# Differences for an adjacency's one-hots: formed on GpSimd for two chunks at once, squared on ScalarE in one instruction

## What is computed

```python
def sage_conv(x, edge_index, W_l, b_l, W_r):
    src, dst = edge_index
    agg = segment_sum(x[src], dst, num_segments=x.shape[0])
    cnt = segment_sum(ones, dst, num_segments=x.shape[0])
    return (agg / max(cnt, 1)[:, None]) @ W_l.T + b_l + x @ W_r.T

x = x + sage_conv(relu(sage_conv(layernorm(x), ...)), ...)     # two graph layers
x = x + ffn(layernorm(x))      # router, spatial and temporal attention, cross attention, MLP
```

## Time and profile before

| | |
|---|---|
| time, median of 3 runs | 1835.78 us (1834.69 to 1836.27) |
| the profiled execution | 1835.89 us |
| its span, first to last instruction | 1833.8 us |
| mean granted TensorE clock | 0.961 |
| busy share: TensorE / weight load / VectorE / ScalarE / GpSimd | 91% / 75% / 61% / 48% / 40% |
| chain that ended last, by engine | PE 73%, DVE 11%, ACT 5%, POOL 4%, issue 3%, DMA 3% |
| the stage of the 83 groups | about 51.5 to 157.6 us |

### The profile page before, as it was taken

The page is one execution under the profiler, slowest core; times in us unless marked ns, Lnnn a source line. Parts: engine busy times, 40 slices in busy tenths (PEclk is TensorE's granted clock), DMA queues, the critical chain, the costliest instruction groups (busy, mean ns, idle before and its releaser), DMA issues.

```text
span 1833.8 us, 27123 instructions
## 1 busy us (share of the span) xinstructions
PE 1659.9 (91%) x9904; PEld 1376.7 (75%) x9904; DVE 1126.7 (61%) x1802; ACT 882.2 (48%) x1728; POOL 725.0 (40%) x593
## 2 busy tenths in 40 slices
PE   2898999849999999988999997999999997699997
PEld 1566776438788888866878996778888885488876
DVE  7995124630588889851048887228888886843332
ACT  3894322312388788722127775108888774311100
POOL 3122020033634455032367873354535556433431
PEclk9998999969999999988999998999999998899999
DMA  3000000131212112033123321321112120011111
GB/s 105 7 24 24 0 29 18 61 131 39 47 29 57 29 29 52 1 97 136 34 60 65 62 53 64 107 62 29 29 34 52 35 80 18 18 35 40 40 40 56
DMA packets 33000, 88.40 MB, mean 48 GB/s; under 512 B 5190, under 2 KB 5660, under 8 KB 32369
## 3 DMA queue, kind: packets, MB, share of 16 engines
q1 hardware_dynamic: 32881, 86.83, 17.3%
HBM read 43.29 MB, written 12.80 MB: 31 GB/s over the span
## 4 chain that ended last, share of the span: by engine, by line
PE 73%; DVE 11%; ACT 5%; POOL 4%; issue 3%; DMA 3%; DVEq 1%; SPq 0%; POOLq 0%; ACTq 0%
PE ps L902 11%; PE ps L687 11%; PE ps L688 11%; PE ps L689 11%; PE ps L883 10%; PE ps L868 7%; PE ps L869 6%; PE ps L808 2%; DMA w_raw<-in_weights 1%; PE ps L809 1%; DVE R L1341 1%; DVE stats L1298 1%; POOL F L604 1%; PE ps L918 1%; ACT F L1077 1%
## 5 line engine op out<-in xcount | busy, mean ns | idle before, releaser
L549 POOL TENSOR_TENSOR w_hi<-w_raw,zero 128x512 fp32r<-128x512 f32 x96 | 109.7, 1142 | 723.8 <-PE ps L689 456.0
L1090 ACT ACTIVATE R<-ps 125x500 fp32r<-125x500 f32 (+3 forms) x632 | 291.1, 508 | 148.1 <-PE ps L883 146.7
L1542 DVE TENSOR_REDUCE TB<-ps 125x1 f32<-125x1250 f32 (+4 forms) x240 | 299.4, 1262 | 83.0 <-PE ps L869 57.4
L1551 DVE TENSOR_TENSOR R<-ps,R 125x500 fp32r<-125x500 f32 (+3 forms) x632 | 324.0, 568 | 11.0 <-ACT R L1090 10.9
L1077 ACT ACTIVATE F<-ps,TB 125x1250 f32<-125x1250 f32 (+4 forms) x240 | 275.9, 1157 | 88.6 <-DVE TB L1542 88.6
L902 PE MATMUL ps<-R 125*128 125x252 f32 (+1 forms) x2080 | 288.7, 286 | 2.3 <-DVE F L1594 2.3
L883 PE MATMUL ps<-ident,F 125*125 125x125 f32 x2040 | 259.9, 275 | 8.4 <-ACT F L1077 7.3
L902 PEld LDWEIGHTS ps<-R 125*128 125x128 f32 x2080 | 255.8, 189 | 2.6 <-DVE R L1551 1.6
L687 PE MATMUL ps<-R,w_hi 128*128 128x512 f32 (+1 forms) x576 | 213.5, 371 | 42.6 <-POOL w_lo L564 14.0
L883 PEld LDWEIGHTS ps<-ident,F 125*125 125x125 f32 x2040 | 239.9, 190 | 11.8 <-ACT F L1077 11.5
L868 PE MATMUL ps<-R 128*125 128x512 f32 (+5 forms) x624 | 240.6, 386 | 4.2 <-DVE R L1551 2.9
(11 more groups left out here) (175 smaller groups left out, 2457.5 us busy)
## 6 DMA issues: line engine op xcount, KB each, us to landing
R<-F SPq DMA_DIRECT2D x96, 312.5 KB, 5.2
w_raw<-in_weights SPq DMA_DIRECT2D x96, 256.0 KB, 2.6
TB<-in_x SPq DMA_DIRECT2D x10, 250.0 KB
x_d<-F SPq DMA_DIRECT2D x10, 250.0 KB
zt_d<-F SPq DMA_DIRECT2D x1, 2500.0 KB, 8.6
F<-zt_d SPq DMA_DIRECT2D x1, 2500.0 KB, 13.1
qc_d<-F SPq DMA_DIRECT2D x4, 625.0 KB, 3.9
xt_d<-F SPq DMA_DIRECT2D x4, 625.0 KB, 3.5
```

Of the source, the lines that this page charges most:

```text
L549: return eng.tensor_tensor(to, a, zero[0:to.shape[0], :].to_broadcast(list(to.shape)), ALU.add)
L1090: eng.activation(probs_run(K, n, 0, part, lo, hi), ps[0:P, 3 * (n % 2) + bank, P * (lo - j0):P * (hi - j0)] .rearrange("p (c t) -> p c t", ...
L1542: ins = eng.tensor_reduce(out=ngm[0:P, 2 * (n % 2) + part:2 * (n % 2) + part + 1], in_=flat(n % 2)[0:P, at:at + P * blocks], op=ALU.max, a ...
L1551: eng.tensor_tensor(probs_run(K, n, 1, part, lo, hi), ps[0:P, 3 * (n % 2) + bank, P * (lo - j0):P * (hi - j0)] .rearrange("p (c t) -> p c ...
```

## The change

GpSimd forms the difference (position + loT) for both chunks of a group in one instruction of 125x2x128, from two broadcast inputs, and writes it as bf16 to `sq_lo`. ScalarE squares it in place, both chunks in one instruction of 256 columns, and goes on as before. GpSimd's addition for group g waits until ScalarE's one-hots of group g-2 have freed the buffer (`lo_ready`); ScalarE's square waits for the addition (`lo_away`, new). The cuts of units 4 to 9 are now placed between the additions: units 4 to 7 behind those for groups 38 to 41, units 8 and 9 behind those for groups 78 and 79; the cuts from unit 10 on come after the last addition.

```diff
+        unit_ok, lo_away = sem("unit_ok"), sem("lo_away")
 @ gpsimd
             eng.memset(F[0:P, 0:5120], 0.0).then_inc(at_zero, 1)
-            cut_units(4, UNIT["us"])
+            def distances(g):
+                if g >= 2:
+                    eng.wait_ge(lo_ready, g - 1)
+                    eng.sem_inc(held, 1)
+                eng.tensor_tensor(sq_lo[:, g % 2, :, :], iota_b[:, 0:128].unsqueeze(1).to_broadcast([P, EA, 128]),
+                                  loT[:, EG * g:EG * g + EA].unsqueeze(2).to_broadcast([P, EA, 128]), ALU.add
+                                  ).then_inc(lo_away, 1)
+            eng.wait_ge(e.ev, 2)
+            eng.sem_inc(held, 1)
+            eng.wait_ge(sp["x"].lo, KC)
+            eng.sem_inc(held, 1)
+            for g in range(NG):
+                distances(g)
+                if 38 <= g < 42 or 78 <= g < 80:
+                    cut_unit((g + 2) // 40 * 4 + (g + 2) % 40, (g + 2) % 4)
+            cut_units(10, UNIT["us"])
 @ scalar
             def squares(g):
-                if g >= 2:
-                    eng.wait_ge(lo_ready, g - 1)
-                for c in range(EA):
-                    ins = eng.activation(sq_lo[:, g % 2, c, :], iota_b[:, 0:128], ACT.Square,
-                                         bias=loT[:, EG * g + c:EG * g + c + 1])
-                ins.then_inc(lo_sq, 1)
+                eng.wait_ge(lo_away, g + 1)
+                away = sq_lo[:, g % 2, :, :].rearrange("p g c -> p (g c)")
+                eng.activation(away, away, ACT.Square).then_inc(lo_sq, 1)
```

More of the change, by code:

```diff
@@ L390, in gnn_ffn_program @@
                              "biasq", "mask_ok", "ysum", "zt_st", "held"))
-        unit_ok = sem("unit_ok")
+        unit_ok, lo_away = sem("unit_ok"), sem("lo_away")
         def inverse_part(K, part):
```

## The result

The changed kernel takes 1890.01 us (median of 4 runs, 1887.42 to 1895.01) beside 1835.24 for the kernel before: ratio 1.0302, 95% interval 1.0279 to 1.0325. The forecast was 1895.0, range 1880 to 1913. Measured again later on another chip, beside the kernel before at 1839.24, it took 1888.7: ratio 1.0270 (1.0256 to 1.0284). The loss is thus 49 to 55 us.

What follows compares the result with a forecast made beforehand. ScalarE and VectorE, not hidden behind TensorE, were taken to bound the stage. 82 x 1.84 less 96.8 gave +54.1; with +1.5, +6.5, +3.5 and -6.5, +59.1 on 1835.89: 1895.0 us, range 1880 to 1913.

Steps and rivals of the forecast that it cites:

- The ring: In the adjacency stage, addition, square, one-hot and next addition follow strictly, one round per group: 1.76 us.
- Contention: Every fourth group VectorE's extra row makes GpSimd's addition wait about 0.3 us: 0.08 per group on average, giving 1.84.
- Pauses: Weight cuts between additions add 6.5 us at groups 38 to 41 and 3.5 at groups 78 and 79.
- Start and end: First one-hot ends 1.5 us later; last adjacency addition comes 1.1 us after the last one-hot, not 7.6: -6.5.
- After the stage: Everything behind the stage waits for its last group and moves by the same amount.
- The signs: GpSimd and ScalarE wait mutually; one-hots 1.75 to 1.95 us apart; TensorE below 65%; last addition 1.1 us after last one-hot.
- (1): TensorE falls to its lower clock level in the stage, pace about 1.99 us per group: +12, 1907 us; chance 0.13.
- (2): GpSimd's bf16 addition takes 0.45 us (1881 in all) or 0.80 (1910) instead of 0.62; together chance 0.12.
- (3): GpSimd's additions and VectorE's one-hots meet in every group: 1911 us, or 1934 at the full loss; chance 0.08.
- (4): The ring does not close, GpSimd works a group ahead and the kernel is not slower: 1826 us; chance 0.03.

Runs made afterwards that it cites:

- e1: The changed kernel with ScalarE issuing each group's square and one-hot in turn, not the next square ahead of the one-hot; 1854.11 us, ratio 1.0069.
- e2: The changed kernel with three buffers of squares in place of two, order of instructions unchanged; 1857.47 us, ratio 1.0086.
- e5: The changed kernel without the semaphore increment between GpSimd's wait for ScalarE and its addition; 1879.61 us, ratio 1.0224.
- e6: The changed kernel with VectorE's extra row cut to 16 columns in the first ten tiles; 1894.10 us, ratio 1.0301.
- e10: The changed kernel with VectorE's extra row cut to 16 columns in the first ten tiles and taken one group later; 1894.09 us, ratio 1.0304.
- e8: The changed kernel with sixteen buffers and GpSimd's additions for groups 0 to 39 only, ScalarE squaring as before from group 40; 1841.47 us, ratio 1.0016.
- e9: The kernel before, with a GpSimd memset of 650 f32 columns beside it in place of each addition, read by nobody; 1836.34 us, ratio 0.9995.
- e4: The kernel before, with the change's GpSimd additions beside it into buffers nobody reads, cuts at the change's places; 1852.47 us, ratio 1.0065.
- e3: The changed kernel with sixteen buffers of squares in place of two, order unchanged; 1858.69 us, ratio 1.0102.
- e7: The changed kernel with sixteen buffers, cuts of units 4 to 7 behind group 50's addition, the rest behind the last; 1853.35 us, ratio 1.0081.

## Why the prediction was right, step by step

- **The ring** was right in kind: the waits, the chain, and e1, e2 and e5 each show it. In size it was 1.76 us undisturbed in the forecast and 1.64 in the trace. The addition is as said (0.61 beside 0.62, the f32 row of equal shape carried over to bf16), the way back too (0.18 beside 0.17). Too long were the square, which gives way to the one-hot after 0.32 us and not 0.40, and the way from GpSimd to ScalarE, 0.04 and not 0.08. I had taken half of two small squares as a floor and added to it; the single instruction, which has no per-partition bias any more, is not bound to that.
- **Contention** was put at 0.08 per group and measured 0.10, so the pace was 1.742 where 1.84 was said. Times 76 that is 7.4 us of the 9.0 by which the stage was overestimated. Its cause was half right: VectorE's lateness at every fourth group, but in the first half not because its row takes long (e6), but because it waits for ScalarE's copy (e10). And GpSimd does not wait before the addition, as said; the addition itself lasts 1.04 us.
- **Pauses**: six long steps sum to 21.3 us, forecast 6 x 1.84 + 10 = 21.0. Right in sum and place; singly they are off by up to 0.4 us (3.66, 3.71, 3.31, 3.25, 4.07 and 3.30, where 3.9 was said for the first of each pause and 3.3 for the others).
- **Start and end**: the first one-hot came 0.4 us later and not 1.5; the last step took 0.4 and not 1.84, since nothing is left to square ahead of it (1.4 us that the sum had not seen); the end was 1.7 behind it and not 1.1. Together with the pace, 59.1 - 7.4 - 1.1 - 1.4 + 0.3 + 0.6 = 50.1, the measured one.
- **After the stage** the forecast had nothing; it was 1.4 us in the profiled execution, the balance of larger parts. The shift falls by 1.1 in the first 250 us behind the stage, grows by 2.4 between 1129 and 1242 us of the kernel before, and by 1.0 behind 1532. The 2.4 go with TensorE's granted clock (two stretches of the kernel before, then the same two after; columns as in the earlier trace rows):

```profile
1138.00:1155.00 17.00, 13.08 (x44) 9.32 (x45) 10.29 (x5) 3.34 (x4) 9.75 (x5) 0.65 0.90 319
...
1176.00:1184.00 8.00, 5.70 (x31) 4.74 (x31) 1.46 (x1) 1.27 (x2) 0.94 (x2) 1.00 0.12 35
```
```profile
1187.00:1205.70 18.70, 14.46 (x44) 10.35 (x45) 10.33 (x5) 3.65 (x4) 10.08 (x5) 0.59 0.88 308
...
1226.70:1236.30 9.60, 7.29 (x32) 5.86 (x31) 1.46 (x1) 1.31 (x2) 0.98 (x2) 0.82 0.09 29
```

  The same jump of 2.4 to 3.4 us is in ten of the thirteen traces, and not in those of the kernel before, e8 and e9. With one trace of most kernels it stays open whether it comes with a kernel or with an execution. The medians differ by 54.8 in the first comparison and 49.5 in the second, while the stage is equal to 0.1 us in both traces of the change; where those 5 us lie stays open too.
- **The signs** that I had named: the waits of GpSimd and ScalarE came as said. The one-hots came 1.74 us apart on average, just below the 1.75 to 1.95. The last addition to the adjacency came 1.7 us behind the last one-hot and not 1.1. TensorE's share in the stage was 70%, not below 65%.
- **Rivals.** (1) TensorE's lower level: it came only in the pauses and for some 7 us behind the first (0.62 from 120 to 135 us), and the rounds behind the pause took 1.64 to 1.66 us all the same. (2) A different duration of the bf16 addition: no, 0.61. (3) A meeting in every group: GpSimd's addition was lengthened in every fourth only. In other rounds VectorE's L1459 met it and lasted up to 0.50 instead of 0.28 us, which VectorE had the time for. (4) A ring that does not close: e1 and e2 made that case on purpose. My price for it was 10 us less than the kernel before; the opened ring measured 14.5 us more (e1). I had let the additions go free of charge and the cuts keep their place; opened, the ring still leaves a loss, from the additions beside VectorE's one-hots (9.8 us between e4 and e9) and from where the cuts stand (8.4 us between e3 and e7).

## What to carry to other kernels

Before handing a step to an idle engine, write down the circle of waits, with each engine's issue order in it: two buffers give no overlap if the consumer issues the next producer-dependent instruction ahead of the one that frees the buffer. The price of a closed ring is the sum of all links, pauses of 0.04 to 0.18 us included; here single rows gave it to some 7%. And an idle engine is not free capacity: look at what else is in its queue (here cuts that wait for TensorE), and at whom it disturbs. When you compare variants, measure the pace at the last engine of the chain: an engine that may run ahead shows a pause late, or not at all.

## What the runs showed of the hardware

- A GpSimd addition of 125x256 takes 0.61 us with bf16 input and output and broadcast inputs, the same as with f32.
- VectorE's one-hot operations (two bf16 inputs from SBUF) and GpSimd's additions hold each other up: the one held up lasted up to 0.43 us longer here (1.04 for 0.61 on GpSimd, started in the same moment; 0.99 for 0.56 on VectorE, started 0.05 us behind). A GpSimd memset of 0.64 us did not disturb them (563 ns in e9, 657 in e4 beside additions). VectorE's addition from PSUM (0.35 to 0.37 us) was not lengthened by either.
- ScalarE started the one-hot, which did not depend on the square ahead of it, 0.32 us after that square of 256 bf16 columns, for which the profile shows 0.42.
- TensorE had the granted clock 1.00 from 60 to 110 us, busy 70%. From 120 to 135 us it had 0.62 on average, busy 7.98 of 15 us.
